# Split operands in the routed stage, a scan over pairs of steps, and a tail and masks moved in between

## The reference

```python
# routed layer: Wg = Wu = Wd = ctx_2048 (4 experts of 256 x 256)
for e in range(4):
    g = silu(einsum('bsd,fd->bsf', h, Wg[e])); u = einsum('bsd,fd->bsf', h, Wu[e])
    y = einsum('bsf,df->bsd', g * u, Wd[e])
    out = where((expert_ids == e)[..., None], y, out)
# recurrence: 256 steps, state h of [256, 16] for each of 4 sequences
x_proj = x @ proj_in_w.T + proj_in_b; delta = softplus(x_proj @ B_w.T); sigA = sigmoid(A)
def step(h, (x_t, d_t)):
    h = h * sigA + x_t[:, :, None] * d_t[:, None, :]
    return h, h.sum(axis=1) @ C_w.T + D_param * x_t
# latent attention: keys of token s count only if seg_id - 8 <= k <= seg_id
good = (k_ids <= qs) & (k_ids >= qs - 8)
scores = where(good, scores, -1e30); attn = softmax(scores)
```

## Time and profile before

| | |
|---|---|
| median of 3 runs | 761.37 us (759.41 to 766.36) |
| profiled execution, device time | 763.71 us |
| its span in the trace | 761.9 us |
| busy: PE, VectorE (DVE), ACT, POOL | 698.1, 485.4, 305.6, 318.7 us |

### The profile page before, as it was taken

How to read it: one execution, slowest core, us unless ns; L and a number is a source line. 1 busy time by engine, 2 the same in 40 slices (tenths; PEclk the granted TensorE clock), 3 DMA queues, 4 the chain that set the end, 5 groups by cost and what they waited for, 6 DMA issues and landing times.

```text
span 761.9 us, 12253 instructions
## 1 busy us (share of the span) xinstructions
PE 698.1 (92%) x4554; PEld 534.4 (70%) x4554; DVE 485.4 (64%) x928; ACT 305.6 (40%) x716; POOL 318.7 (42%) x453
## 2 busy tenths in 40 slices
PE   5989899999999898777999999999979999999993
PEld 4856564685666565435877787877858888888883
DVE  4478764331135789975998988882455656565656
ACT  3655523102211845122767776771142222222220
POOL 4323316400101769402766666662243445544521
PEclk9999999999799999887999999999979999999998
DMA  7000006001002000000000000003010111121001
GB/s 261 1 2 3 2 2 274 1 0 42 1 1 78 1 18 1 1 1 0 2 1 1 2 1 2 2 0 105 1 41 22 52 54 42 43 63 42 1 0 56
DMA packets 10460, 23.28 MB, mean 31 GB/s; under 512 B 2081, under 2 KB 5218, under 8 KB 10018
## 3 DMA queue, kind: packets, MB, share of 16 engines
q1 hardware_dynamic: 10402, 22.50, 8.9%
HBM read 21.45 MB, written 1.05 MB: 30 GB/s over the span
## 4 chain that ended last, share of the span: by engine, by line
PE 74%; DVE 18%; ACT 4%; issue 3%; DMA 1%; POOL 0%; POOLq 0%; DVEq 0%; SPq 0%; ACTq 0%
PE psum L394 30%; PE psum L427 8%; DVE A L1259 7%; PE psum L914 6%; PE psum L945 4%; PE psum L646 4%; PE psum L923 3%; PE psum L450 3%; PE psum L729 2%; PE psum L501 2%; PE psum L543 1%; DVE probs L1103 1%; DVE A L1170 1%; PE psum L507 1%; PE psum L407 1%
## 5 line engine op out<-in xcount | busy, mean ns | idle before, releaser
L394 PE MATMUL psum<-parts 128*128 128x256 f32 (+2 forms) x1440 | 255.8, 337 | 13.5 <-DVE parts L1124 8.7
L394 PEld LDWEIGHTS psum<-parts 128*128 128x128 f32 (+1 forms) x1440 | 221.4, 194 | 45.6 <-DVE parts L1124 8.7
L1710 POOL TENSOR_SCALAR probs<-probs,row_rec 128x256 f32<-128x256 f32 x128 | 60.8, 489 | 55.0 <-DVE row_rec L1114 53.9
L1433 ACT ACTIVATE probs<-probs,neg_max 128x256 f32<-128x256 f32 x128 | 64.0, 503 | 40.4 <-DVE neg_max L1107 40.4
L1259 DVE TENSOR_TENSOR_SCAN A<-decay,psum 128x256 f32<-128x256 f32 x128 | 75.0, 660 | 5.4 <-PE psum L774 5.4
L1660 ACT ACTIVATE A<-psum 128x512 f32<-128x512 f32 x44 | 26.3, 598 | 129.6 <-PE psum L394 129.6
L1380 DVE TENSOR_TENSOR A<-A,psum 128x512 f32<-128x512 f32 x44 | 30.2, 687 | 70.2 <-PE psum L394 70.2
L1826 POOL CAST parts<-C 128x512 fp32r<-128x512 f32 (+1 forms) x44 | 31.1, 707 | 100.5 <-PE psum L394 90.1
L914 PE MATMUL psum<-C,A 128*128 128x256 f32 x256 | 69.6, 396 | 0.0
L1827 POOL TENSOR_TENSOR parts<-C,parts 128x512 fp32r<-128x512 f32 (+1 forms) x44 | 54.9, 1247 | 3.5
L914 PEld LDWEIGHTS psum<-C,A 128*128 128x128 f32 x256 | 44.8, 194 | 15.6 <-issue 10.7
(11 more groups left out here) (206 smaller groups left out, 1191.1 us busy)
## 6 DMA issues: line engine op xcount, KB each, us to landing
C<-in_experts SPq DMA_DIRECT2D x22, 384.0 KB, 3.1
A<-in_w_o SPq DMA_DIRECT2D x1, 2048.0 KB, 12.0
x_tok<-in_x_tok SPq DMA_DIRECT2D x1, 1024.0 KB, 6.9
ctxT<-in_ctxT SPq DMA_DIRECT2D x1, 1024.0 KB, 10.4
out<-x_tok SPq DMA_DIRECT2D x8, 128.0 KB, 1.8
A<-in_w_uqT SPq DMA_DIRECT2D x1, 768.0 KB, 6.0
xT<-in_xT SPq DMA_DIRECT2D x2, 256.0 KB, 4.4
C<-in_wqk SPq DMA_DIRECT2D x1, 512.0 KB, 5.8
```

Of the source, the lines that this page charges most:

```text
L394: ins = mm(o, left[l], right[r], start=first and n == 0, stop=last and n == 2, skip_group_check=True)
L1433: last = af(slot, scores, ACT.Exp, bias=neg_max[:, u % RING[n], j:j + 1], accum_out=row_sum[:, u % RING[n], j:j + 1])
L1710: last = pool.tensor_scalar(pr, pr, row_rec[:, u % RING[n], j:j + 1], 1.0, ALU.mult, ALU.mult)
```

## The change

Routed stage: ctx and x are split into parts, so an up is six single-pass matmuls and an output tile 24; each hidden tile gets a rounded copy (ACT, `high_of`) and a low part (VectorE, `low_of_hidden`) behind the mask product, which now goes to a ring of four buffers. The output tiles of the first half come after up 10, those of the second half between the logits' halves. POOL splits ctx during the first attention.

Scan: ACT copies the even columns out of the bank (`even_out`), VectorE adds them, decayed, to the odd ones in place (`combine`, every second column of PSUM), and scans 128 pairs with the squared decay; the even steps' sums come from the state before, decayed, and a fresh term (`fresh_sums`). POOL takes a third token tile in odd units. Placement in the units shifts by some numbers.

Tail: the first four query pairs go behind units 29 to 31 and the loop's end; the first scores wait only for scan 61; `state_sums(7)`, `outputs(1)`, `merge(1)`, the output tiles 4 to 7, their LayerNorm and `query_latents(1)` go into steps 1 to 11. Query pairs 4 to 31 go into the even steps from 4.

Masks: ACT squares the distance, VectorE makes the mask in one operation (four from the middle: over 20 instead of 16).

```diff
+        hid_parts0 = view(A_rounded, 0, [P, 8, 2, HALF])
+        hid0 = view(free_T, 0, [P, 4, HALF])
+        ctx_parts = view(parts, 4096, [P, 2, B * DC, 256])
...
+        PAIRS = S // 2
...
+        FIRST = 4
+        QUERIES_AT = {2 * (n - FIRST) + 4: n for n in range(FIRST, B * NPAIR)}
+        TURNS_AT, LATENTS_AT = {6: 2, 9: 3}, 11
...
-            for k in range(16):
+            def up(k):
                 half, e, fc = k // 8, k // 2 % 4, k % 2
-                if k == 8:
-                    ln_transposes(0, 1)
+                o, hh = bank[k % 4][:, :], slice(half * HALF, (half + 1) * HALF)
                 pe.wait_ge(sem("ln_xT"), 2 * (half + 1))
                 if k >= 4:
                     pe.wait_ge(sem("r_mul"), k - 3)
-                proj(bank[k % 4][:, :], ctxT[:, e], fc * P, half).then_inc(sem("r_up"), 1)
+                for r in range(2):
+                    for c in range(DC):
+                        mm(o, ctx_parts[:, r, DC * e + c, fc * P:(fc + 1) * P], x_parts[:, 0, c, hh],
+                           start=(r == 0 and c == 0), stop=False)
+                pe.wait_ge(sem("r_xlo"), 2 * (half + 1))
+                for c in range(DC):
+                    last = mm(o, ctx_parts[:, 0, DC * e + c, fc * P:(fc + 1) * P], x_parts[:, 1, c, hh],
+                              start=False, stop=(c == DC - 1))
+                last.then_inc(sem("r_up"), 1)
             def out1(i, o):
-                pe.wait_ge(sem("r_hid"), 8 * (i // 4 + 1))
+                pe.wait_ge(sem("r_lo"), 8 * (i // 4 + 1))
                 for k in range(8):
-                    last = mm(o, hid0[:, k, i * P:(i + 1) * P], ctxT[:, k // 2, k % 2, :],
-                              start=(k == 0), stop=(k == 7))
+                    last = product3(o, [hid_parts0[:, k, r, (i % 4) * P:(i % 4 + 1) * P] for r in range(2)],
+                                    [ctx_parts[:, r, k, :] for r in range(2)], k == 0, k == 7)
                 return last
-            close(1, out1)
+            pe.wait_ge(sem("r_ctx"), 4)
+            for k in range(11):
+                if k == 6:
+                    ln_transposes(0, 1)
+                up(k)
+            final(1, range(4), out1)
+            for k in range(11, 16):
+                if k == 14:
+                    ln_transposes(1, 0)
+                up(k)
...
             hidden(0)
             low_rank(0)
             low_rank(1)
+            logits(0)
+            final(1, range(4, NT), out1)
+            low_rank(2)
+            low_rank(3)
             ln_transposes(1, 1)
             hidden(1)
-            pe.wait_ge(sem("f_hT"), 4)
...
-            low_rank(2)
-            low_rank(3)
+            logits(1).then_inc(sem("f_lg"), 1)
...
+                if n == 29:
+                    pe.wait_ge(sem("q_split"), 3)
+                    pe.wait_ge(sem("operand_lo"), QC_AT + 1)
+                if n >= 29:
+                    query_pair(n - 29)
+            query_pair(3)
+            def next_queries(u):
+                n = QUERIES_AT.get(u)
+                if u == 1:
+                    state_sums(7)
+                    outputs(1)
+                if u in (2, 3):
+                    if u == 2:
+                        pe.wait_ge(sem("q_mul"), 3)
+                    final(3, (2 * u, 2 * u + 1), out3)
+                if u == min(QUERIES_AT):
+                    pe.wait_ge(sem("ln_r"), 8 * 3 + NT)
+                if u in TURNS_AT:
+                    if u == 9:
+                        pe.wait_ge(sem("a4_oT"), 1)
+                    ln_transposes(3, 1, (TURNS_AT[u],))
+                if u == 9:
+                    pe.wait_ge(sem("ln_xT"), 4 * 3 + 3)
+                if u == LATENTS_AT:
+                    pe.wait_ge(sem("a4_oT"), 2)
+                    query_latents(1)
+                if u == LATENTS_AT + 2:
                     pe.wait_ge(sem("operand_lo"), QC_AT + 2)
+                if n is not None:
+                    query_pair(n)
...
-            query_pair(0)
-            outputs(1)
-            query_pair(1)
-            pe.wait_ge(sem("q_mul"), 1)
-            final(3, range(4, NT), out3)
-            query_pair(2)
-            pe.wait_ge(sem("q_lat"), 3)
-            ln_transposes(3, 1)
-            query_latents(1)
-            pe.wait_ge(sem("q_mul"), 3)
+            pe.wait_ge(sem("s_scan"), 2 * SCAN_UNITS - 2)
...
+            def low_of_x(q):
+                dve.wait_ge(sem("ln_xT"), q + 1)
...
+                tt(four(x_parts[:, 1, :, cols]), ln_bank(0, q)[:, :].rearrange("p (i c t) -> p c i t", i=2, c=2),
+                   four(x_parts[:, 0, :, cols].bitcast(f32)), ALU.subtract).then_inc(sem("r_xlo"), 1)
...
+            def product_of(k):
                 dve.wait_ge(sem("r_silu"), k + 1)
-                tt(hid0[:, k % 8, half * HALF:(half + 1) * HALF], silu0[:, k % 4, :], bank[k % 4][:, :],
-                   ALU.mult).then_inc(sem("r_mul"), 1)
-            norm(1, 1.0, fin_bank)
+                if k >= 4:
+                    dve.wait_ge(sem("r_lo"), k - 3)
+                tt(hid0[:, k % 4, :], silu0[:, k % 4, :], bank[k % 4][:, :], ALU.mult).then_inc(sem("r_mul"), 1)
+            def low_of_hidden(k):
+                dve.wait_ge(sem("r_hi"), k + 1)
+                tt(hid_parts0[:, k % 8, 1, :], hid0[:, k % 4, :], hid_parts0[:, k % 8, 0, :].bitcast(f32), ALU.subtract
+                   ).then_inc(sem("r_lo"), 1)
+            for k in range(10):
+                product_of(k)
+                if k == 6:
+                    low_of_x(2)
+                    low_of_x(3)
+                if k >= 2:
+                    low_of_hidden(k - 2)
+            product_of(10)
+            for i in range(4):
+                residual(1, i, 1.0, fin_bank)
+            product_of(11)
+            low_of_hidden(8)
+            for i in range(4):
+                normalise(1, i)
...
+            def combine(m):
+                n, c = m // 2, m % 2
+                q, half, j = scan_unit(n)
+                dve.wait_ge(sem("s_even"), m + 1)
+                u = bank[m % 4][:, :].rearrange("p (k r) -> p r k", r=2)
+                stt(u[:, 1, :], even_u[:, m % 4, :], decay[:, c, 4 * q + j:4 * q + j + 1], u[:, 1, :], ALU.mult, ALU.add
+                    ).then_inc(sem("s_comb"), 1)
...
                 for b in range(2):
-                    at = slice(b * S, (b + 1) * S)
+                    u = bank[m % 4][:, b * S:(b + 1) * S].rearrange("p (k r) -> p r k", r=2)
                     last = dve.tensor_tensor_scan(
-                        hs[:, G % 2, c, j, at], decay[:, c, 4 * q + j:4 * q + j + 1].broadcast_to([P, S]),
-                        bank[m % 4][:, at], 0.0, ALU.mult, ALU.add)
+                        hs[:, G % 2, c, j, b, 1:PAIRS + 1],
+                        decay2[:, c, 4 * q + j:4 * q + j + 1].broadcast_to([P, PAIRS]), u[:, 1, :],
+                        0.0, ALU.mult, ALU.add)
                 last.then_inc(sem("s_scan"), 1)
...
             def window_mask(i):
-                link(ts(distance, iota4, seg_f[:, i:i + 1], None, ALU.subtract))
-                link(tt(distance, distance, distance, ALU.mult))
-                ts(mask_m[:, i, :], distance, 16.0, NEG, ALU.is_gt, ALU.mult).then_inc(sem("mask"), 1)
-                dve.wait_ge(sem("mask"), i + 1)
+                dve.wait_ge(sem("squared"), i + 1)
+                ts(mask_m[:, i, :], distance[i % 2], 20.0, NEG, ALU.is_gt, ALU.mult).then_inc(sem("mask"), 1)
...
+            step_done(0)
+            combine(0)
+            for m in range(2 * SCAN_UNITS):
+                n = m // 2
+                if m + 1 < 2 * SCAN_UNITS:
+                    combine(m + 1)
+                scan(m)
+                if m == 26:
+                    step_done(1)
+                if m == 37:
+                    merge(0)
+                if m == 41:
+                    residual3(0)
+                    residual3(1)
+                if m == 43:
+                    residual3(2)
+                    residual3(3)
+                if m == 47:
+                    for i in range(4):
+                        normalise(3, i)
+                if m == 57:
+                    query_low(0)
+                    loaded(dve, "tab_qc", "tab_qs")
+                if m in (60, 62):
+                    rotate_pair((m - 60) // 2)
...
+                if m in (51, 53):
+                    window_mask((m - 51) // 2)
...
+                if u == 1:
+                    merge(1)
+                if u in (2, 3):
+                    for i in (2 * u, 2 * u + 1):
+                        residual3(i)
+                if u in (5, 7):
+                    for i in (u - 1, u):
+                        normalise(3, i)
+                if u in MASKS_AT:
+                    window_mask(MASKS_AT[u])
+                if u == LATENTS_AT:
+                    query_low(1)
...
+            def silu_of(k):
                 act.wait_ge(sem("r_up"), k + 1)
                 if k >= 4:
```

(65 more changed lines are left out.)

451 lines of the change are left out of this document (241 added, 210 removed).

## The result

| | before | after |
|---|---|---|
| median of 19 runs | 762.54 us (759.41 to 766.36) | 756.73 us (748.47 to 760.26) |
| ratio | | 0.9908, 95% interval 0.9887 to 0.993 |
| profiled execution, span | 763.71, 761.9 | 756.73, 754.8 |

0.9% faster, where 3% were forecast: 756.73 lies outside the range of 730 to 754.

What follows compares the result with a forecast made beforehand. TensorE was taken to bound the routed stage and latent attention, VectorE the scan, nothing the stretch between scan and first latent score. Gains 5 + 3 + 11 + 3 = 22 us gave 740 us, range 730 to 754.

Steps and rivals of the forecast that it cites:

- Routed stage: Routed experts: split single-pass matmuls save TensorE time; gain taken as 5 us (0 to 9).
- low part and mask take turns: Routed stage: VectorE's low part and POOL's mask product exclude each other, 1.16 + 0.69 = 1.85 us a tile.
- Scan: Scan stage: 128 pair scans and 64 combines, stage 84.5 us against 87.2; gain taken as 3 us (-4 to +10).
- step pair: Scan: one combine at 0.38 us and two scans at 0.32 make 1.02 us; 64 make 65.3, 9.7 less.
- ring stalls 6 (0 to 11): Scan: VectorE stalls when other work exceeds the four PSUM banks' slack of 0.8 us; 6 us in all.
- a sign of being wrong: Scan: VectorE idle over 12 us for ACT or PE would show the forecast wrong.
- The start of the scan: Scan: the first combine stands behind two scalings and a projection on ACT, 1.4 us.
- the 3.0 moved in from the tail: Scan: VectorE gets two query rotations, two masks and the fresh sums from the tail, 3.0 us added.
- Rival 3: Scan: the ring governs, 11 us of stalls, combine 0.416, scan 0.35 (6.1 more); 751 us in all; chance 0.14.
- Tail: Last scan to latent attention: early query pairs move into the scan's PE gaps; gain taken as 11 us (6 to 15).
- E + 37: Tail: queries of step 12 stand about 37 us after E, the last scan's end.
- Masks: Latent attention: one-operation masks on VectorE, squares on ACT, keep the 4.89 us pace; gain 3 us.

Runs made afterwards that it cites:

- whole_scan: The changed kernel with the scan, state sums and outputs of before (256 steps, no combine, no even copies, scalings two each for ACT and POOL): 750.43 us.
- routed_only: The kernel before with only the new routed stage, by halves with split operands; scan, tail and masks as before: 757.2 us.
- tail_order: The changed kernel with ACT's even copies ahead of scalings, plus reciprocal deviations of tiles 4 to 7 and the latents' low part moved in the tail: 748.14 us.
- ring5: The changed kernel with a fifth PSUM bank in the scan's ring for steps 32 to 56: 756.11 us.
- result_in_sbuf: The changed kernel with the combine's result written over the even columns in SBUF, read there by the scan, the bank returned at the combine's end: 770.7 us.
- copies_first: The changed kernel with ACT's two copies of the even columns placed before the scaling of the later unit, not behind it: 749.95 us.

## Why the prediction was wrong, step by step

**Routed stage: right.** Forecast 5, measured 5.6. Two details differ. I let low part and mask take turns, 1.85 a tile. They did lengthen each other (1.16 and 0.69 alone), but by less than strict turns: the mask took 1.44 and the low part 0.90 on average in the first half, so ups came 1.36 apart and the first output tile 19.84 us after the first up (129.04 - 109.20), not 21.55 (the terms written there add up to 133.9, not 134.5). Folds 8 us earlier instead of 6.3; the half clock then took about 3 back, which I had put at up to 5. These rows carry the first detail:

```profile
L1320 DVE TENSOR_TENSOR A_rounded<-probsT,A_rounded 128x512 fp32r<-128x512 f32 x8 | 7.2, 896 | 0.0
...
L1950 POOL TENSOR_TENSOR probsT<-probsT,C 128x512 f32<-128x512 f32 x11 | 15.6, 1442 | 3.7 <-DVE probsT L1315 3.6
```

**Scan: the step that failed.** Its prices were nearly right: issued back to back a step pair takes 1.01 to 1.04, forecast 1.02, and 7.5 us of VectorE's work were saved where 9.7 were forecast; that the two kernels differ by 9.5 is luck, from normalisations that took longer in `whole_scan`. What failed is the term "ring stalls 6 (0 to 11)" and the account beneath it. I compared a bank's way back, 1.2 us, with VectorE's 2.04 between uses, and let PE's other work and three table loads eat the slack of 0.8; ACT's other work I checked by its sum ("under 84 each"). But ACT works in order, and its share of the way back isn't 0.38: it is the copy plus whatever stands before it, 0.9 for two scalings, 1.2 for the key latents' copies, 1.28 for a table load. Stalls came to 13.3, of which 8.7 go with the copies; that VectorE waits over 12 us for ACT was a sign of being wrong that the prediction had named. The start of the scan, put at 1.4, was 2.7. A third error is in the base: I added the 3.0 moved in from the tail in full, while before VectorE stood for 3.7 between first and last scan (81.8 busy of 85.4), and most of what VectorE got more to do went in there (87.1 with 86.8 busy). The pairs by themselves, forecast 5.7 better (87.2 + 3.0 - 84.5), were 6.2 worse: 7 of the 11.9 by stalls, 1.3 by the start, 3.4 by the base. Rival 3 had the place, the sign and, with 11 us, nearly the size, but 6.1 of its 11 were dearer prices, which did not come, and of its stalls it named only the ring's small slack, not what stands in ACT's queue. How much a larger ring would have saved stays open.

**Tail: mechanism right, size off.** Scores followed the last scan at once. The whole scan shows the tail without the pairs: from last scan's end to the output tiles 173.4, `routed_only` 182.2. That is 8.8 for tail and masks where 14 was forecast. The queries of step 12 came at E + 42.9 there, not E + 37. I had counted PE's stop for the deviations as 3.5 with the pace going on behind it; the latents' turn in step 11, VectorE held for a copy in ACT's queue, I had not. With both moved it was E + 37.8, at a full clock (in `tail_order`, at 0.93, E + 40.1), so the forecast's E + 37 also took a full clock for granted: with the old order `ring5` reached E + 40.7 at 0.96. In the profile of after the first scores also ran at the half clock (3.41 us for eight records, clock 0.83 from 336 to 352), and step 12 came at E + 44.8.

**Masks: right.** Queries 4.89 apart from 381.14 on, no step longer: 3.

**The sum.** 5.6 from the routed stage, 6.8 from tail and masks with what they moved into the scan (757.2 to 750.43), -6.3 from the pairs (750.43 to 756.73): 6.1, against 5.8 measured. This is no test of the terms: each is the difference of two neighbouring medians, so they must add up, and each is known to 2 or 3 us. The forecast had 22. The chance of 0.86 for faster by over 1% leaned on four gains being independent; one of them turned round.

## What to carry to other kernels

When work is moved off a busy engine at the price of a copy on an engine with room, price the copy's place in that engine's order, not its length or the engine's sum: a ring's slack has to cover everything that stands before the hand-over. Put the copy that a ring waits for ahead of work that is made in advance. And price moved-in work against the idle time of the stage as it is, before adding it in full.

## What was not expected of the hardware

- A scan's price falls with its columns almost like an elementwise operation's: 0.403 us mean for 128 columns against 0.658 for 256, and reading every second column of PSUM costs nothing that shows (`result_in_sbuf`, unit stride from SBUF, POOL still: 0.73 for two, as 0.72 to 0.73 from PSUM).
- With both inputs in SBUF the same two scans take 1.62 to 2.07 us beside a GpSimd instruction.
- Raising the clock of a stage from 0.92 to 0.98 with added matmuls made the stage 2.4 us longer (93.03 for 90.58), not shorter; the matmuls themselves added 7.8 us of PE's work.
- One kernel's tail, with the same order of work, took 4.0 us less at a granted clock of 0.96 over its first 40 us than at 0.85 (`ring5` and the changed kernel).
- Why the combine can't take both columns from PSUM, which would spare the copy: the Trainium skill, "PSUM — Partial Sum Buffer", section "Specifications (TRN2)", allows a VectorE instruction one tensor input from PSUM. No run here shows it.

Left open: what a fifth bank would spare in steps 0 to 31; how the 4.6 us divide that VectorE still stands without any copies (PE's other work and the half clock); how the tail's 4.2 us divide between the two waits and the clock; and why the median of `copies_first` moved more than its trace, beyond the clock.
